# Two-layer attention and LoRA-expert block on one core: rows of score maxima turned among the next step's slots, copied by ScalarE

## The reference

```python
qkv = layernorm(x) @ Wqkv            # 32 query heads of 16, one key head, one value head
scores = einsum("bqhd,bkd->bhqk", q, k) * 0.25
scores = where(causal, scores + slope[h] * (pos_k - pos_q), -1e30)
x = x + einsum("bhqk,bkd->bqhd", softmax(scores), v).reshape(2, 1024, 512) @ Wo
n = layernorm(x)
x = x + n @ W_base.T + b_base + top-2-of-8 LoRA experts of rank 16 (n)
```

## Time and profile before

| | |
|---|---|
| median of 3 runs | 700.57 us (700.55 to 702.18) |
| profiled execution | 700.96 us, its span 699.2 us |
| PE busy | 669.7 us, 96% of the span |
| DVE busy | 557.4 us, 80% |
| ACT busy | 358.6 us, 51% |
| POOL busy | 216.9 us, 31% |
| granted TensorE clock | full in every slice |

### The profile page before, as it was taken

One profiled execution on the slowest core, in us unless ns is written; L12 is line 12 of the kernel. 1 busy time (PEld: TensorE's weight loads), 2 busy tenths in 40 slices (PEclk: granted clock), 3 DMA queues, 4 the chain that ended last, 5 costly groups with the idle time before them and its releaser, 6 DMA issues.

```text
span 699.2 us, 13261 instructions
## 1 busy us (share of the span) xinstructions
PE 669.7 (96%) x4304; PEld 305.5 (44%) x4304; DVE 557.4 (80%) x1801; ACT 358.6 (51%) x511; POOL 216.9 (31%) x366
## 2 busy tenths in 40 slices
PE   3889999999999999999999999999999999999997
PEld 2434344544344444444443343433433455555553
DVE  5899889887989889898988989899881365666565
ACT  2324647567556676666666666767667411111111
POOL 0035424233332515243352231422432412222220
PEclk9999999999999999999999999999999999999999
DMA  8578108080411443080144744225200189700001
GB/s 253 130 145 137 64 2 136 30 147 28 166 54 51 60 89 108 11 131 34 41 63 94 102 81 77 49 49 94 48 18 33 52 130 170 162 30 30 31 30 60
DMA packets 42951, 56.32 MB, mean 81 GB/s; under 512 B 6648, under 2 KB 26232, under 8 KB 42752
## 3 DMA queue, kind: packets, MB, share of 16 engines
q1 hardware_dynamic: 40296, 51.27, 37.3%
q10 hardware_dynamic: 2592, 4.26, 1.8%
HBM read 35.72 MB, written 19.79 MB: 79 GB/s over the span
## 4 chain that ended last, share of the span: by engine, by line
PE 83%; DVE 10%; DMA 3%; ACT 2%; issue 1%; SPq 1%; POOL 0%; DVEq 0%; ACTq 0%; POOLq 0%
PE psum L780 20%; PE psum L732 18%; PE psum L762 13%; PE psum L808 8%; PE psum L830 7%; PE psum L678 7%; PE psum L759 5%; DVE psum L1145 3%; PE psum L825 2%; PE psum L840 2%; ACT work L965 2%; DMA x_sb<-in_x 1%; DVE negm L1150 1%; PE psum L817 1%; DMA arena<-q_dram 1%
## 5 line engine op out<-in xcount | busy, mean ns | idle before, releaser
L965 ACT ACTIVATE work<-psum 128x1024 f32<-128x1024 f32 (+1 forms) x320 | 289.0, 943 | 127.6 <-PE psum L762 108.5
L1145 DVE CUSTOM_DVE_ANT_0 psum<-psum,future 128x384 f32<-128x384 f32 (+3 forms) x512 | 237.7, 514 | 12.6 <-PE psum L732 10.4
L732 PE MATMUL psum<-k_op,arena 106*128 106x512 bf16 (+3 forms) x768 | 212.4, 328 | 9.6 <-DVE negm L1145 4.3
L1150 DVE TENSOR_REDUCE negm<-psum 128x1 f32<-128x512 f32 x256 | 168.6, 687 | 15.3 <-PE psum L732 10.9
L1318 POOL TENSOR_SCALAR_AFFINE_SELECT work<-work 128x512 f32<-128x512 f32 x128 | 81.2, 634 | 296.2 <-ACT work L965 296.2
L780 PE MATMUL psum<-work,v_op 128*32 128x512 f32 (+3 forms) x1536 | 163.5, 498 | 0.5 <-POOL work L1318 0.4
L762 PE MATMUL psum<-arena,k_op 109*128 109x512 bf16 (+3 forms) x640 | 157.3, 316 | 1.9 <-ACT work L965 0.8
L732 PEld LDWEIGHTS psum<-k_op,arena 106*128 106x128 bf16 x768 | 69.0, 97 | 128.5 <-DVE negm L1145 40.7
L678 PE MATMUL psum<-arena,wqkv_sb 128*128 128x256 f32 (+3 forms) x240 | 84.6, 453 | 1.1 <-ACT arena L887 1.1
L759 PE MATMUL psum<-arena,k_op 116*128 116x128 bf16 x512 | 84.3, 221 | 0.9 <-ACT work L965 0.9
L762 PEld LDWEIGHTS psum<-arena,k_op 109*128 109x128 bf16 x640 | 59.6, 98 | 44.5 <-ACT work L965 15.7
(11 more groups left out here) (86 smaller groups left out, 454.8 us busy)
## 6 DMA issues: line engine op xcount, KB each, us to landing
arena<-q_dram SPq DMA_DIRECT2D x96, 128.0 KB, 5.5
o_dram<-o_sb SPq DMA_DIRECT2D x32, 256.0 KB
q_dram<-arena SPq DMA_DIRECT2D x16, 384.0 KB, 4.4
arena<-o_dram SPq DMA_DIRECT2D x32, 128.0 KB, 4.6
arena<-rcp_dram SPq DMA_DIRECT2D x32, 128.0 KB, 4.9
out<-wqkv_sb ACTq DMA_DIRECT2D x16, 256.0 KB, 2.0
x_sb<-in_x SPq DMA_DIRECT2D x3, 1024.0 KB, 10.0
work<-in_x SPq DMA_DIRECT2D x3, 1024.0 KB, 18.8
```

The costliest lines, as they stand in the source:

```text
L732: last = nc.tensor.matmul(bank[:, a * width:(a + 1) * width], q_op[0:ROW_MAX, bass.ds(col, P)], k_op[0:ROW_MAX, b, k0:k0 + width], start=T ...
L965: nc.scalar.activation(probs[:, n % 4, heads * hp:heads * (hp + 1), 0:w], src, ACT.Exp).then_inc(exp_done, 1)
L1145: last = nc.vector.tensor_tensor_reduce(keys, keys, future[:, CH - width:CH], -1.0, 3e38, ALU.add, ALU.min, negm[:, late, 0, j * QT + t:j ...
L1150: nc.vector.tensor_reduce(dst, psum[:, bank, 0:len(js) * width].rearrange("p (a k) -> p a k", a=len(js)), AX_X, ALU.max, negate=True).then ...
```

## The change

The two `turn` slots leave the list, which then has 40 entries, and become pieces of their own in PE's order with semaphores of their own (`turn_full`, `turn_done`). The early unit's turn stands behind slot 14. The late unit's turn stands behind slot 2 of the next step (for the last group, ahead of step 16), and waits until all slots of its own step are finished. ACT instead of DVE copies the turned bank to `m_t`. A late diag slot starts its minimum from the column that the full slot wrote, given to the custom instruction as a per-partition operand, and waits for that full slot; the separate minimum goes. The planner no longer counts DVE time for turns.

```diff
-TURN_AFTER = 3
+TURN_AFTER = (3, 3)
-SLOTS.insert(TURN[0], ("turn", 0, None, None))
-SLOTS.insert(TURN[1], ("turn", 1, None, None))
...
-    time = 450 if kind == "turn" else 680 if kind == "full" else (550, 750, 500, 700)[t]
+    time = 680 if kind == "full" else (550, 750, 500, 700)[t]
...
+def turn_behind(k, put):
+    if put == EARLY_SLOTS + TURN_AFTER[0]:
+        return [("turn", 2 * k, None)]
+    if put == TURN_AFTER[1] and k:
+        return [("turn", 2 * k - 1, None)]
+    return []
...
-        while k < NK and put < NSL - 1 and slot_due(k, put) * total <= done:
+        while k < NK and put < NSL and slot_due(k, put) * total <= done:
             out.append(("slot", k, put))
             put += 1
+            out += turn_behind(k, put)
...
+            elif what == "turn":
+                bank = banks.pop(0)
+                turn_at[a] = (bank, last[bank])
+                last[bank] = ("turn", a)
+                banks.append(bank)
...
+            def turn_maxima(u):
+                bank, before = TURN_BANK[u]
+                bank_free(before)
+                pe.wait_ge(slot_free, NSL * (u // 2) + (NSL if u % 2 else EARLY_SLOTS))
+                nc.tensor.transpose(psum[0:UH * QT, bank, 0:P], negm[:, u % 2, 0, :], ident[:]).then_inc(turn_full, 1)
...
+            def copy_maxima(u):
+                act.wait_ge(turn_full, u + 1)
+                if u >= 2:
+                    act.wait_ge(m_split, u - 1)
+                nc.scalar.copy(m_t[:, u % 2], psum[0:UH * QT, TURN_BANK[u][0], 0:P]).then_inc(turn_done, 1)
...
                     if kind == "diag":
                         if late:
+                            dve.wait_ge(slot_free, NSL * k + SLOTS.index(("full", 1, t, js[-1:])) + 1)
                         for a, j in enumerate(js):
                             keys = psum[:, bank, a * width:(a + 1) * width]
-                            last = nc.vector.tensor_tensor_reduce(keys, keys, future[:, CH - width:CH], -1.0, 3e38, ALU.add, ALU.min,
-                                                                  negm[:, late, 0, j * QT + t:j * QT + t + 1])
+                            at = j * QT + t
+                            last = nc.vector.tensor_tensor_reduce(keys, keys, future[:, CH - width:CH], -1.0,
+                                                                  negm[:, 1, 1, at:at + 1] if late else 3e38, ALU.add, ALU.min,
+                                                                  negm[:, late, 0, at:at + 1])
...
             def split_max(u, i):
-                pool.wait_ge(slot_free, at_loop(NSL * (u // 2) + TURN[u % 2] + 1, i, 2 * NSL))
+                pool.wait_ge(turn_done, u + 1)
```

More of the change, by code:

```diff
@@ L217, in pe_order @@
         done += w
-        while k < NK and put < NSL - 1 and slot_due(k, put) * total <= done:
+        while k < NK and put < NSL and slot_due(k, put) * total <= done:
             out.append(("slot", k, put))
             put += 1
+            out += turn_behind(k, put)
         out.append(piece)
-    return out + [("slot", k, r) for r in range(put, NSL if k < NK else 0)]
+    for r in range(put, NSL if k < NK else 0):
+        out.append(("slot", k, r))
+        out += turn_behind(k, r + 1)
+    return ([("turn", NU - 1, None)] if k == NK else []) + out
 ORDER = [pe_order(k) for k in range(NK + 2)]
 def places():
-    slot_at, use_at, last = {}, {}, [None] * NSB
+    slot_at, use_at, turn_at, last = {}, {}, {}, [None] * NSB
     for u in range(N_FIRST):
@@ L267, in uses_behind @@
             piece = b
-        if what == "side" and b == len(use_parts(USES[a])) - 1:
-            out.setdefault(piece, []).append(a)
+        if what == "turn" or what == "side" and b == len(use_parts(USES[a])) - 1:
+            out.setdefault(piece, []).append((what, a))
     return out
@@ L653, in bank_free @@
                     pe.wait_ge(slot_free, n + 1)
+                elif what == "turn":
+                    pe.wait_ge(turn_done, n + 1)
                 else:
@@ L707, in max_slot @@
                 bank = psum[:, bank]
-                if kind == "turn":
-                    if late:
-                        pe.wait_ge(max_late, k + 1)
-                    else:
-                        pe.wait_ge(slot_free, NSL * k + EARLY_SLOTS)
-                    nc.tensor.transpose(bank[0:UH * QT, 0:P], negm[:, late, 0, :], ident[:]).then_inc(slot_full, 1)
-                    return
                 b, g, s = k // NB, (k % NB) // 2, k % 2
@@ L792, in step @@
                         max_slot(m, n)
+                    elif what == "turn":
+                        turn_maxima(m)
                     elif what == "scores":
@@ L922, in copy_values, with evict @@
                 nc.scalar.copy(v_op[:, QT * c:QT * (c + 1), 1, DH:VW], v).then_inc(side_free, 1)
+            def copy_maxima(u):
[3 more added lines that the diff above has]
+                nc.scalar.copy(m_t[:, u % 2], psum[0:UH * QT, TURN_BANK[u][0], 0:P]).then_inc(turn_done, 1)
+            def evict(what, n):
+                if what == "side":
+                    side(n)
+                else:
+                    copy_maxima(n)
             def side(u):
@@ L947, in _ @@
                     rstd_first(2)
-            for u in range(len(BEFORE), N_FIRST):
-                side(u)
+            for piece in uses_behind(0).get(None, ()):
+                evict(*piece)
             def exps(m, n, i, behind):
@@ L965, in exps @@
                     nc.scalar.activation(probs[:, n % 4, heads * hp:heads * (hp + 1), 0:w], src, ACT.Exp).then_inc(exp_done, 1)
-                    for u in behind.get((n, hp), ()):
-                        side(u)
+                    for piece in behind.get((n, hp), ()):
+                        evict(*piece)
                     if hp == 0 and n == LAG - 1 and m:
@@ L983, in step @@
                 behind = uses_behind(k)
-                for u in behind.get(None, ()):
-                    side(u)
+                for piece in behind.get(None, ()):
+                    evict(*piece)
                 for n in range(NTI):
@@ L1117, in _, with step @@
             KEY_PIECES = 7
-            def step(k, i=None, some=range(NSL)):
+            def step(k, some=range(NSL)):
                 for r in some:
@@ L1136, in step @@
-                    dve.wait_ge(slot_full, at_loop(idx + 1, i, 2 * NSL))
-                    width = P * (t + 1) if kind == "diag" else CH
-                    where = 1 if kind == "full" else 0
-                    if kind == "diag":
-                        if i is not None:
-                            dve.nop(nofuse=True)
+                    if k and r in (0, EARLY_SLOTS):
+                        dve.wait_ge(turn_full, 2 * k - 1 + late)
+                    dve.wait_ge(slot_full, idx + 1)
@@ L1169, in _ @@
             for r in range(NSL):
-                step(0, None, (r,))
+                step(0, (r,))
                 if r in KEY_SLOTS[0]:
@@ L1175, in _ @@
             for r in range(NSL):
-                step(1, None, (r,))
+                step(1, (r,))
                 if r in STAT_SLOTS:
@@ L1182, in _ @@
                 for r in range(NSL):
-                    step(k, None, (r,))
+                    step(k, (r,))
                     if r in KEY_SLOTS.get(k, ()):
```

23 lines of the change are left out of this document (8 added, 15 removed).

## The result

The changed kernel takes 705.83 us in the median (704.49 to 706.57, 4 runs), the kernel before 701.38 in runs beside it (700.55 to 702.23, 4 runs): a ratio of 1.0061, 95% interval [1.0038, 1.0084]. The forecast was 705.1, slower; that holds. In later runs the ratio was 1.0054 [1.0035, 1.0073]. The profiled execution took 704.49, its span is 702.7. Runs of the kernel before with a mean granted clock of 0.997 or less took 0.8 to 2.3 us longer in the median than the others of the same batch, so a ratio to it depends in part on how many such runs it holds.

A forecast was written before the change was run, and what follows sets the result against it. PE was taken as the bound, with 83% of the chain of waits. 3.3 - 1.2 + 2.0 + 0.4 = 4.5 us on 700.96 gives 705.5, median 705.1; range 699.5 to 709.5, the forecast's own 702.7 to 707.5.

The forecast's parts named there:

- The late turn: At 15 step ends: turn waits for DVE to finish slot 0, first scores 0.22 us later, 3.3 us more.
- Slot 11: In six steps without projections, PE's wait for DVE at slots 9 to 11, about 0.2 us, goes: 1.2 us back.
- The early turn: In steps 5 to 9 slot 15 waits 0.40 us for the bank of slot 14: 2.0 us more.
- The operand: Per-partition operand in 16 late diag instructions: 0.064 us each; 0 for steps 2 to 15, 0.4 us for step 1.
- The added waits: Late diag slots' waits for a full slot are met when asked: 0; asked directly behind it, 23 us.
- ScalarE's copies: Two ACT copies a step of about 0.28 us each, expected to cost 0.
- The loaded rows: Split, store and load after the late copy come 1.0 us later; 3.2 of 4.2 us stay: cost 0.
- the 1.35 us of the earlier trace that I called DVE's own loss: At a step's end DVE sits idle 1.35 us until PE's turn; said to cost PE only 0.32 us.
- Rival B: No change: the longer wait at the turn is given back later in the step; some +1, 701.6 us; chance 0.27.
- A: Faster: PE reaches the late turn after slot 0 is done, both waits go; some 6 us, 694.6; chance 0.14.
- C: Much slower: the per-partition operand makes DVE the bound in the late part; 713 or 708 us; chance 0.11.
- D: Late diag slots' added waits are not met when asked; a tenth of 23 us gives 707; chance 0.03.

## Why the prediction was right, point by point

From slot 0 of step 0 to the end the change costs 4.4 us, and the forecast's sum was 4.5. The mechanism of both turns was right, and the closeness of the sum is partly luck. By stretch the terms of the forecast come to 1.3 us in steps 0 to 4, 3.1 in steps 5 to 9 and 0.1 from step 10 on; the runs gave 1.95, 3.15 and -0.7, so two misses cancel. By cause: 4.8 for the late turns and 2.0 for the early ones, less 1.1 at slot 11, less 0.5 for a wait that went later in steps 5 to 9, less 1.65 for the reciprocals of step 11; the 0.8 or so that is left is what steps 0 to 4 grew by beyond their late turns.

- **The late turn.** Right in kind, too small: first scores 1.20 us behind slot 0 instead of 0.88, 0.32 a step end and not 0.22, some 4.8 us and not 3.3. The step that failed is "0.33" from PE's start to DVE's: with two waits in front it took 0.43, and with the waits in the other order the turn came 0.98 behind slot 0, the number worked out.
- **Slot 11.** Right: 0.18 gone in six steps. The rest of the late part came to nothing: waits at slots 27 and 32 (0.11 and 0.16) for those of 0.10 and 0.17 that the kernel before had at its slots 33 and 38.
- **The early turn.** Right to the hundredth: 0.40 in each of steps 5 to 9. That those steps are 0.63 longer where 0.6 was said is luck: the late turn took 0.1 more than forecast there, and a wait of 0.10 at the kernel before's slot 32 went.
- **The operand.** Cheaper in each instruction, 0.04 to 0.05 us instead of 0.064, but the run without it gained 2.3 us in all, where 0.4 was said. Of these 0.9 is the collision in step 0 that falls away with it, not the operand itself. "0 for steps 2 to 15" held from step 5 on within 0.1 a step; step 0 was left out of the count.
- **The added waits.** Right: in front of the 256 late diagonal instructions no idle time of DVE over 0.04 us ended with a full slot. A late diagonal instruction starts as far ahead of the recorded end of the slot before it as an unconditional one, 383.07 against 381.87 + 1.29 = 383.16:

```profile
381.87 1.29 DVE L1179 TENSOR_REDUCE negm<-psum 128x1 f32<-128x512 f32 x2
383.07 0.75 DVE L1173 CUSTOM_DVE_ANT_0 psum<-psum,future,negm 128x512 f32<-128x512 f32 x1
```

The section of the Trainium skill that the prediction set against the trace here (VectorE: DVE Perf Modes, "The DRAIN you can't avoid") goes on to say that a next operation which is not held starts earlier. A start 0.09 us ahead of the recorded end is therefore no disagreement with it.

- **ScalarE's copies.** Right, 0, from step 5 on: the copies on VectorE gave the same periods there.
- **The loaded rows.** Right from step 2 on: PE does not wait for them there. In step 1 a wait went that the kernel before had.
- **Not seen.** Step 11 gained 1.5 us (1.65 without its late turn and slot 11), because the 1.35 us of the earlier trace rows that I called DVE's own loss were in front of the reciprocals in one step. Step 0 lost 1.2 to GpSimd, and step 1 gained 0.8; that is 0.45 in sum, of which 0.32 is the late turn. Step 2 lost 1.9: 0.32 for its late turn and 1.3 around its early turn (0.29 at the turn, 0.54 at slot 15, 0.49 at slot 18). With the pieces in their old places 0.46 went; the cause of the rest is open, and so is what made steps 3 and 4 0.35 shorter in spite of their late turns.

Rival B fell with steps 5 to 9, A with the turn that PE always reaches before slot 0 is done, C with the run without the operand, D with the idle times and rows under the added waits.

## What to carry to other kernels

A small piece of work put into a ring of buffers costs what the ring's next free buffer costs: ask which reduction that buffer waits for, not how long the piece takes. Put such a piece where its own input is long ready and a long instruction stands behind it (ahead of the last value product), not among slots that are issued back to back. An engine's idle time in front of a wait is free only until some step has work queued behind that wait: look for the one step in sixteen that does. And what a step gains counts only up to the next wait: the 1.8 us that a later turn saved in step 0 were mostly waited for in step 1, where the loaded rows were not there yet.

## What the runs showed of the hardware

- A second semaphore wait in front of an instruction on VectorE cost 0.10 us when the wait asked last was the one already met (0.43 us from PE's start to DVE's at slot 0), and nothing in the other order (0.32; a slot with one wait took 0.33). At slot 12 it was 0.07 (0.49 and 0.42).
- A normalisation of 128 x 512 values on VectorE took 0.52 to 0.55 us alone and 0.72 to 1.52 beside GpSimd's two-input work. The Trainium skill (SBUF — State Buffer, "SBUF: two separate sides") says that the two engines share a port pair under an exclusive lock, that an operation of VectorE takes part in it in a 2-port mode or with two inputs in SBUF, that whichever engine starts first keeps the pair for its instruction, and that the other is blocked. The trace does not name the mode of the normalisation. It agrees on the size (one tile 1.0 us longer beside an operation of 1.16), and the loser changes with a shift of 0.1 us: in the run without the operand the tile was recorded 0.17 ahead of GpSimd's operation, took 0.54, and GpSimd's took 1.38 instead of 1.16. That the first to start wins the recorded starts alone do not show, since in the changed kernel the tile was recorded 0.08 ahead (50.09 and 50.17) and was the one that lasted.
- In two of the profiles PE's granted clock was 0.50, its level of 1.2 GHz, for 3 us of step 0, and then full again, which cost about 1.4 us; ahead of it PE had been busy for 2.67 of 4.30 us. In the other profiles the same stretch kept its clock, also where PE was busy as little (1.39 of 3.00 us from 43.5 on in the run with the waits in the other order). Two stretches of the run with the moved reciprocals (columns as in the earlier trace rows):

```profile
40.00:44.30 4.30, 2.67 (x7) 0.59 (x5) 4.27 (x8) 1.21 (x2) 2.48 (x3) 1.00 1.13 296
44.30:47.40 3.10, 2.85 (x5) 1.49 (x6) 2.06 (x7) 0.01 (x1) 0.00 (x0) 0.50 0.64 113
```
